# First four stages of part 0: gathered rows replaced by rows picked with one-hot matmuls (recommendation tower, 32 features)

## What is computed

```python
e = jnp.stack([tbl_0[ids[:, 0]], ..., tbl_31[ids[:, 31]]], axis=1)      # 2048 x 32 x 64
z = concatenate([sum(e, -1), einsum('bpd,pde,bpe->bp', e[:, II], kernels, e[:, JJ])], 1)   # 32 + 496
h = concatenate([z, dense_ctx], 1)
h = relu(h @ W_top1 + b_top1)      # 544 -> 512
h = relu(h @ W_top2 + b_top2)      # 512 -> 256
y = h @ W_top3                     # 256 -> 1
```

## Time and profile before

| what | value |
|---|---|
| median of 3 runs | 814.21 us (813.42 to 814.73) |
| the profiled execution | 812.35 us |
| its span, first to last instruction | 810.5 us |
| TensorE busy (PE) | 761.7 us, 94% |
| VectorE busy (DVE) | 720.8 us, 89% |
| ScalarE busy (ACT) | 681.7 us, 84% |
| GpSimd busy (POOL) | 607.3 us, 75% |
| bytes by indirect DMA, by plain DMA | 16.81 MB, 10.63 MB |

### The profile page before, as it was taken

How to read it: one execution, slowest core, us unless ns; L and a number is a source line. 1 busy time by engine, 2 the same in 40 slices (tenths; PEclk the granted TensorE clock), 3 DMA queues, 4 the chain that set the end, 5 groups by cost and what they waited for, 6 DMA issues and landing times.

```text
span 810.5 us, 20371 instructions
## 1 busy us (share of the span) xinstructions
PE 761.7 (94%) x6000; PEld 458.4 (57%) x6000; DVE 720.8 (89%) x684; ACT 681.7 (84%) x5282; POOL 607.3 (75%) x966
## 2 busy tenths in 40 slices
PE   0378989999999999999999999999999999999998
PEld 0144435565565666666666666656565665656656
DVE  0268999998999989999999989999999999999891
ACT  1057899989979999789989899799997899798993
POOL 6775888888888888888888888888868888660000
PEclk9999999999999999999999999999999999999999
DMA  4545111111111111111111111111111111110000
GB/s 136 162 134 181 27 24 26 25 26 25 26 26 25 26 25 25 26 25 25 25 27 25 25 25 26 25 25 26 24 23 24 26 25 26 20 21 2 1 2 1
DMA packets 20014, 28.74 MB, mean 35 GB/s; under 512 B 9024, under 2 KB 9664, under 8 KB 19008
## 3 DMA queue, kind: packets, MB, share of 16 engines
q0 software_dynamic: 16384, 16.81, 10.7%
q1 hardware_dynamic: 3520, 10.63, 4.0%
HBM read 27.40 MB, written 0.01 MB: 34 GB/s over the span
## 4 chain that ended last, share of the span: by engine, by line
PE 83%; DMA 6%; POOL 6%; issue 2%; ACT 2%; DVE 1%; DVEq 0%; POOLq 0%
PE m_ps L646 25%; PE m_ps L662 25%; PE acc L676 13%; PE tr L585 8%; DMA gathered<-in_tbl,idx 6%; POOL gathered L328 6%; PE tr L566 4%; PE tr L599 3%; ACT turned_act L427 1%; PE m_ps L648 1%; PE m_ps L585 1%; PE tr L580 1%; PE m_ps L599 0%; POOL x_half L311 0%; DMA idx<-in_ids 0%
## 5 line engine op out<-in xcount | busy, mean ns | idle before, releaser
L427 ACT ACTIVATE turned_act<-turned_act 128x64 f32<-128x64 f32 x2560 | 612.1, 244 | 26.3 <-DVE turned_act L513 26.2
L328 POOL DMA_INDIRECT gathered<-in_tbl,idx x512 | 489.4, 956 | 100.2 <-issue 74.4
L427 ACT ACTIVATION_READ_ACCUMULATOR turned_act<-turned_act 128x1 f32 x2560 | 486.4, 190 | 0.0
L488 DVE TENSOR_TENSOR prod<-m_ps,x_t 128x1024 f32<-128x1024 f32 x256 | 308.1, 1217 | 11.2 <-PE m_ps L648 10.7
L646 PE MATMUL m_ps<-x_t,k_sb 64*128 64x256 f32 x1024 | 271.8, 391 | 3.9 <-DVE turned_act L513 2.1
L648 PE MATMUL m_ps<-x_t,k_sb 64*128 64x256 f32 x1024 | 272.6, 392 | 0.0
L662 PE MATMUL m_ps<-k_sb,x_t 64*128 64x512 f32 x1024 | 262.7, 608 | 4.4 <-DVE turned_act L513 3.5
L646 PEld LDWEIGHTS m_ps<-x_t,k_sb 64*128 64x128 f32 x1024 | 182.4, 188 | 107.9 <-issue 63.2
L513 DVE TENSOR_TENSOR turned_act<-m_ps,gathered 128x1024 f32<-128x1024 f32 x160 | 193.4, 1217 | 25.0 <-PE m_ps L662 12.4
L648 PEld LDWEIGHTS m_ps<-x_t,k_sb 64*128 64x128 f32 x1024 | 182.1, 188 | 0.0
L662 PEld LDWEIGHTS m_ps<-k_sb,x_t 64*128 64x128 f32 x1024 | 92.6, 187 | 67.1 <-issue 43.7
(11 more groups left out here) (36 smaller groups left out, 152.6 us busy)
## 6 DMA issues: line engine op xcount, KB each, us to landing
gathered<-in_tbl,idx POOLq DMA_INDIRECT x512, 2.5
k_sb<-in_kmat SPq DMA_DIRECT2D x7, 1024.0 KB, 4.9
w_sb<-in_w SPq DMA_DIRECT2D x1, 1280.0 KB
k_sb<-in_kmat SPq DMA_DIRECT2D x2, 256.0 KB, 3.1
k_sb<-in_kmat SPq DMA_DIRECT2D x1, 512.0 KB, 5.1
w_sb<-in_w SPq DMA_DIRECT2D x1, 512.0 KB
idx<-in_ids SPq DMA_DIRECT2D x1, 256.0 KB, 2.6
z_sb<-in_dense_t SPq DMA_DIRECT2D x8, 16.0 KB, 2.1
```

The costliest lines, as they stand in the source:

```text
L328: nc.gpsimd.indirect_dma_start(out=gathered[:, t, G % GR, f * D:(f + 1) * D], out_offset=None, in_=tables[2 * (STAGES - 1 - a) + f], in_of ...
L427: last = nc.scalar.activation(row, row, ACT.Copy, accum_out=z_turned[:, q % 2, t, 16 * c + n:16 * c + n + 1])
L488: nc.vector.tensor_tensor(prod[:, r % PR, :, :].rearrange("p u (e n) -> p u e n", e=2), m_ps[:, p % MR, :, :].rearrange("p u (e n) -> p u ...
```

## The change

The rows of stages 0 to 3 of part 0 are no longer gathered. The eight tables are loaded whole, each over 125 partitions with r = 8 or 10 rows per partition (row p x r + c lies in partition p at place c). The 256 indices of a feature are loaded to all 125 partitions (`ids_hot`). For each place c, VectorE compares the indices with p x r + c (`rows_hot`, one float per partition and place) and writes a 125x256 matrix of ones and zeros; TensorE multiplies the 125x64 piece of the table with it and accumulates over c in PSUM. The result is the stage's transposed rows, in `tr` as before: feature 0 in rows 0 to 63, feature 1 in rows 64 to 127. The matrices lie in a ring of five. VectorE makes all 70 before its first product. Tables, lists and matrices lie in parts of `x_t`, `w1_sb` and `z_sb` that are not yet used; the load of `w1_sb` waits until stage 3 is picked. The sums of the four stages' rows come from eight small matmuls with `sel` (`first_sums`), whose result ScalarE copies to `z_nat`. Gathers begin with stage 4 (k = 16); counts of semaphores are adjusted.

```diff
+HOT = 4
+HOT_P = 125
+HOT_RING = 5
+TABLES_AHEAD = 3
...
+AHEAD[0, FIRST_AHEAD[HOT + 2]].append(("s", 0, 0))
...
+SIZES = (125000, 1000, 1000, 1250, 12500, 1000, 1250, 12500, 1250, 1000, 12500, 1250, 125000, 125000, 12500, 12500,
+         1000, 12500, 1000, 1250, 1000, 12500, 12500, 1250, 1000, 1250, 1000, 1000, 1000, 1250, 1000, 1250)
+HOT_R = [[SIZES[2 * (STAGES - 1 - _a) + _f] // HOT_P for _f in range(2)] for _a in range(HOT)]
+HOT_COLUMNS = sorted({(_r, _c) for _pair in HOT_R for _r in _pair for _c in range(_r)})
...
+        K0 = HOT * GATHERS
+        hot_steps = [(a, c, f) for a in range(HOT) for c in range(max(HOT_R[a])) for f in range(2) if c < HOT_R[a][f]]
+        final = {(a, f): max(j for j, e in enumerate(hot_steps) if e[0] == a) for a in range(HOT) for f in range(2)}
+        used_by = [sum(i != final[hot_steps[i][0], 0] for i in range(j + 1)) for j in range(len(hot_steps))]
+        w1_flat = w1_sb[:].rearrange("p k n -> p (k n)")
+        x_flat = x_t[:, STAGES:XR, :].rearrange("p s n -> p (s n)")
+        def hot_table(a, f):
+            home, first = (x_flat, 0) if a < TABLES_AHEAD else (w1_flat, TABLES_AHEAD)
+            at = D * (sum(sum(HOT_R[b]) for b in range(first, a)) + (HOT_R[a][0] if f else 0))
+            return home[0:HOT_P, at:at + D * HOT_R[a][f]]
+        def hot_matrix(j):
+            at = D * sum(HOT_R[HOT - 1]) + QB * (j % HOT_RING)
+            return w1_flat[0:HOT_P, at:at + QB]
+        def hot_ids(a):
+            return z_sb[0:HOT_P, a // 2, a % 2 * 2:a % 2 * 2 + 2, :].bitcast(i32)
...
-                pool.wait_ge(gather_landed[k % IN_FLIGHT], (k // IN_FLIGHT + 1) * 16)
+                pool.wait_ge(gather_landed[k % IN_FLIGHT], ((k - K0) // IN_FLIGHT + 1) * 16)
...
-            for k in range(NQ * STAGES * GATHERS):
+            for k in range(K0, NQ * STAGES * GATHERS):
...
-                if k >= IN_FLIGHT:
+                if k >= K0 + IN_FLIGHT:
...
-                if n == 0 and G >= GR:
+                if n == 0 and G >= GR + HOT:
...
             sp.dma_start(idx[:], ids).then_inc(idx_loaded, 16)
+            sp.dma_start(rows_sb[:], rows_hot).then_inc(rows_loaded, 16)
+            def load_tables(a):
+                sp.dma_start(hot_ids(a), ids_hot[a:a + 1, :].rearrange("o (f n) -> o f n", f=2).partition_broadcast(HOT_P)).then_inc(ids_hot_loaded[a], 16)
+                for f in range(2):
+                    sp.dma_start(hot_table(a, f), tables[2 * (STAGES - 1 - a) + f].rearrange("(p r) d -> p (r d)", p=HOT_P)).then_inc(tables_loaded[a], 16)
+            load_tables(0)
+            load_tables(1)
             sp.dma_start(b1_sb[:], b1).then_inc(small_loaded, 16)
             sp.dma_start(b2_sb[:], b2).then_inc(small_loaded, 16)
             sp.dma_start(w3_sb[:], w3).then_inc(small_loaded, 16)
             at = 0
             for n, size in enumerate(K_LOADS):
+                if n == 1:
+                    load_tables(2)
+                    load_tables(3)
                 if n > 2:
                     sp.wait_ge(tr_kept, 3 * (n - 2) // 2)
                 sp.dma_start(k_sb[:, at:at + size, :], kmat[:, at * P:(at + size) * P].rearrange("p (d n) -> p d n", n=P)).then_inc(k_loaded[n], 16)
                 at += size
+            sp.wait_ge(tr_filled, place("x", 0, HOT - 1))
             sp.dma_start(w1_sb[:], w1.rearrange("(k p) n -> p k n", p=P)).then_inc(weights_loaded, 16)
             sp.dma_start(w2_sb[:], w2.rearrange("(k p) n -> p k n", p=P)).then_inc(weights_loaded, 16)
...
+            def keep_first_sums():
+                act.wait_ge(tr_filled, place("s", 0, 0))
+                nc.scalar.activation(z_nat[:, 0, :, 0:2 * HOT], tr[:, 0, 0:TILES * 2 * HOT].rearrange("p (t n) -> p t n", t=TILES),
+                                     ACT.Copy).then_inc(tr_kept, 1)
...
             def sum_x(q, a, n):
                 G = q * STAGES + a
+                if q == 0 and a < HOT:
+                    return
...
+            dve.wait_ge(rows_loaded, 16)
+            for j, (a, c, f) in enumerate(hot_steps):
+                if c == 0 and f == 0:
+                    dve.wait_ge(ids_hot_loaded[a], 16)
+                if j >= HOT_RING:
+                    i = j - HOT_RING
+                    if i == final[hot_steps[i][0], 0]:
+                        dve.wait_ge(tr_filled, place("x", 0, hot_steps[i][0]))
+                    else:
+                        dve.wait_ge(hot_used, used_by[i])
+                column = HOT_COLUMNS.index((HOT_R[a][f], c))
+                nc.vector.tensor_scalar(out=hot_matrix(j), in0=hot_ids(a)[:, f, :], scalar1=rows_sb[0:HOT_P, column:column + 1],
+                                        scalar2=None, op0=ALU.is_equal).then_inc(hot_ready, 1)
...
+            def pick_rows(a):
+                free_tr("x", 0, a)
+                pe.wait_ge(tables_loaded[a], 32)
+                for j, (b, c, f) in enumerate(hot_steps):
+                    if b == a:
+                        pe.wait_ge(hot_ready, j + 1)
+                        last = nc.tensor.matmul(tr[f * D:(f + 1) * D, 0, :], hot_table(a, f)[:, c * D:(c + 1) * D], hot_matrix(j),
+                                                start=(c == 0), stop=(c == HOT_R[a][f] - 1))
+                        if j == final[a, 0]:
+                            last.then_inc(tr_filled, 1)
+                        else:
+                            last.then_inc(hot_used, 1)
+            def first_sums():
+                free_tr("s", 0, 0)
+                for t in range(TILES):
+                    for a in range(HOT):
+                        at = 2 * (HOT * t + a)
+                        last = nc.tensor.matmul(tr[:, 0, at:at + 2], x_t[:, slot(0, a), t * P:(t + 1) * P], sel[:, 30:32],
+                                                start=True, stop=True)
+                last.then_inc(tr_filled, 1)
...
             def transpose(q, a):
                 G, n = q * STAGES + a, STAGES_AT_ONCE[q]
+                if q == 0 and a < HOT:
+                    pick_rows(a)
+                    return
                 if q == 0:
                     for landed in gather_landed:
-                        pe.wait_ge(landed, (G + n) * GATHERS // IN_FLIGHT * 16)
+                        pe.wait_ge(landed, ((G + n) * GATHERS - K0) // IN_FLIGHT * 16)
                 else:
...
+                if what == "s":
+                    keep_first_sums()
...
+        "ids_hot": np.ascontiguousarray(ids[0:QB, hot].T).reshape(HOT, 2 * QB),
+        "rows_hot": np.array([[p * r + c for r, c in HOT_COLUMNS] for p in range(P)], np.float32),
```

More of the change, by code:

```diff
@@ L203, with dlrm_tower @@
 VECTOR_SUMS_BEHIND = (7, 10, 11, 12, 13, 15, 17, 18, 19, 23, 24, 25, 26, 27, 28, 29, 30, 31)
-def dlrm_tower(nc, ids, tables, kmat, dense_t, w1, b1, w2, b2, w3, out):
+SIZES = (125000, 1000, 1000, 1250, 12500, 1000, 1250, 12500, 1250, 1000, 12500, 1250, 125000, 125000, 12500, 12500,
+         1000, 12500, 1000, 1250, 1000, 12500, 12500, 1250, 1000, 1250, 1000, 1000, 1000, 1250, 1000, 1250)
+HOT_R = [[SIZES[2 * (STAGES - 1 - _a) + _f] // HOT_P for _f in range(2)] for _a in range(HOT)]
+HOT_COLUMNS = sorted({(_r, _c) for _pair in HOT_R for _r in _pair for _c in range(_r)})
+def dlrm_tower(nc, ids, ids_hot, rows_hot, tables, kmat, dense_t, w1, b1, w2, b2, w3, out):
     fp32, i32 = mybir.dt.float32, mybir.dt.int32
@@ L237, in dlrm_tower @@
         y_sb = sb("y_sb", [P, YN])
+        rows_sb = sb("rows_sb", [P, len(HOT_COLUMNS)])
         idx = sb("idx", [P, NQ * STAGES * GATHERS], i32)
@@ L255, in dlrm_tower @@
         small_loaded = sem("small_loaded")
+        rows_loaded = sem("rows_loaded")
+        ids_hot_loaded = [sem(f"ids_hot_loaded{a}") for a in range(HOT)]
+        tables_loaded = [sem(f"tables_loaded{a}") for a in range(HOT)]
+        hot_ready = sem("hot_ready")
+        hot_used = sem("hot_used")
         weights_loaded = sem("weights_loaded")
@@ L401, in keep_z @@
                 nc.scalar.activation(z_sb[:, q % 2, b, :], acc[:, 0:QB], ACT.Copy).then_inc(z_kept, 1)
+            def keep_first_sums():
+                act.wait_ge(tr_filled, place("s", 0, 0))
+                nc.scalar.activation(z_nat[:, 0, :, 0:2 * HOT], tr[:, 0, 0:TILES * 2 * HOT].rearrange("p (t n) -> p t n", t=TILES),
+                                     ACT.Copy).then_inc(tr_kept, 1)
             def keep(what, q, n):
-                if what == "x":
+                if what == "s":
+                    keep_first_sums()
+                elif what == "x":
                     keep_x(q, n)
@@ L459, in sum_x @@
                 G = q * STAGES + a
+                if q == 0 and a < HOT:
+                    return
                 if q == 0:
                     for landed in gather_landed:
-                        dve.wait_ge(landed, (G + n) * GATHERS // IN_FLIGHT * 16)
+                        dve.wait_ge(landed, ((G + n) * GATHERS - K0) // IN_FLIGHT * 16)
                     nc.vector.tensor_reduce(z_nat[:, 0, :, 2 * a:2 * a + 2],
@@ L496, in turned_product @@
```

(11 more changed lines are left out.)

6 lines of the change are left out of this document (3 added, 3 removed).

## The result

| what | before | after |
|---|---|---|
| median of 22 runs each | 813.34 us (810.46 to 815.39) | 815.13 us (812.73 to 818.31) |
| the profiled execution | 812.35 us | 815.48 us |
| its span | 810.5 us | 813.7 us |
| T, start of the first turned product | 49.09 us | 55.44 us |

The ratio is 1.0027, with a 95% interval of 1.0016 to 1.0038: slower by some 2.2 us, where 2.7 us faster was forecast.

The account below looks back on a forecast made before the run. The start-up up to T was taken as the bound: tables at 33.5 us, picking to 41.0, then 8.1 us, left T at 49.1 us, unchanged; the closed gap gave -2.7 us, so 811.5 us by the median, range 801.5 to 818.5.

Parts of the forecast that it names:

- Where the end is set: Start-up: everything behind T, the first turned product's start at 49.09 us, is the same work, so the end moves with T.
- Gap behind T: VectorE's waits between 70.89 and 74.06 us, for stage 11 and then TensorE, 2.75 us in all, would go.
- Contention: Gathers up to stage 11: 10 us allowed for slowing by other loads, within 57 us where 69.7 us would do.
- Compares and matmuls: Picking stages 0 to 3: 70 steps, each a 0.32 us compare and a matmul of 0.24 or 0.47 us.
- the chain behind it: From the end of picking at 41.0 us to T: copies, transposes, sums and multiplies in TensorE's order, 8.1 us.
- rival B: TensorE stays at half speed through stage 3 and the chain to T: T 56.1 us, time 818.5 us; chance 0.15.
- Loads: Start-up lists and tables over 125 rows: five DMA engines at 24 GB/s, stage 3's tables in at 33.5 us (31 to 37.6).
- rival A: Start-up loads use all 16 engines: picking ends at 31.3 us, T 39.4 us, time 801.8 us; chance 0.17.

## Why the prediction was wrong

**Where the end is set** held: what follows T took 758.2 to 758.4 us of the span in the changed kernel and in those with held blocks, lists over 128 and all engines. T -5.8, -8.3 and -12.4 us shortened the spans by 5.8, 8.3 and 12.3 us. With three stages T -18.0 us gave only -15.0 us (13.3 by the ratios), since VectorE waits behind T again.

**Gap behind T** held: no wait for gathers. But stage 4 and later did not come 20 us sooner. The second part's first halving started at 81.29 us, where it had been 94.38 (the chain up to 90 us is gathers in flight to 64.1%, 48.9%). Contention took 7 us; the slack given for it covered that.

**Compares and matmuls** held: 0.305 us for a taken 0.32; half speed for some ten steps and 4.5 us (40.20 to 44.74 us), where 8.5 steps and 4.0 us were forecast; sums 1.95 us for 2.0; stage 3 from start to end 7.2 us for 7.5; the chain behind it 8.06 us for 8.1. The stay at half speed (rival B) did not come: the steps behind 44.74 us are 0.31 us apart again.

**Loads: the step that failed.** "Stage 3's tables are in at 33.5 us (31 to 37.6)" (3.4 + 29.9 is 33.3, a slip of no weight): it was 40.2 us, 6.7 us later, beyond the bound. Of the 6.7 us, 4.76 were the wait of stage 3. The other 1.9 would have been there with tables in time, since TensorE was busy until 35.4 us: its first pick began at 14.28 us, where tables at about 11 us had been worked out. The number of engines, five, and their rate, 24 GB/s, were right. With all engines instead (rival A, as an edit) the time was 803.82 us, for 801.8 worked out; its picking ended at 34.99 us where 31.3 was given, because the first tables came at 8.8 and not 6.6 us, and between the picks of the four stages lay 3.9 us (1.82 and 0.47 us of waits for ScalarE's copies and 1.63 us with the first even step in it), for which 0.6 us had been given; the picks themselves took 22.2 us, 1.8 less than worked out. The Trainium skill ("DMA: Bandwidth & Descriptors", section "Why a DMA increments its semaphore by 16 and not by 1") has the number of engines as the largest up to 16 that divides the slowest dimension on both sides; by it, five for 125 rows, and the packets here agree, with 30 per 0.5 us at 84 ns.

Two sentences of that step were wrong. "SP issues 13 more transfers at 0.43 us each, the last at about 8.4 us: no bound": the last ended at 24.1 us, since SP's issue itself was held while earlier loads lay on the five engines (5.95 us; 1.64 with the lists elsewhere; none with all loads on all engines). What in the queue holds it is not shown. It delays every load that stands behind in SP's order. The start was slow besides: the core moved 93 GB/s in the first 10 us, where the all-engines kernel moved 189; why the first lists and tables ran under their later rate was not tried. And the kernel blocks were taken to lie queued behind the tables; they went beside stage 3's tables, whose packets took 131 ns instead of 84, and cost some 3.5 us by the run that held them back. With those blocks held and the shorter stop of SP the last 2,560-byte packet ends at 34.05 us and stage 3 starts at 34.7 us, 1.2 us over the forecast: in this one execution the sum by bytes nearly comes out, for five engines that are left alone.

With T at 49.1 + 6.35 us the same working gives 809.65 + 6.3 = 816.0 us for the profiled execution, which took 815.48. That the changed kernel's time lay within the range is no merit of the mechanism: it lay there on the side of rival B, by another cause, late tables and not a slow TensorE.

## What to carry to other kernels

Before a load is placed, divide its rows: 125 rows went over five engines, and here a broadcast over 128 partitions instead of 125 gave 8 us back, together with tables loaded as 112 and 13 rows 10.5 us. Cost a load with few engines twice, by its bytes over those engines and by the time for which the queue that issues it is held, and look at what is issued beside it. And with a chain like this one, find the term that decides (here one landing time), and let its bounds cover what the loads before and beside it can do to it, not only the spread of its own rate.

## What the runs showed that was not expected

- An issue of SP took up to 3 us (5.95 us for two) instead of 0.43 us when earlier loads lay on five engines. The same two tables as four loads on more engines took 1.70 us.
- The stop of SP is not the same in every execution: 5.95 us in one and 4.10 us in another, with the same code up to there.
- TensorE's granted clock fell after short idle time: in the changed kernel TensorE idled from 35.4 to 40.2 us, and the granted clock is 1.00 up to 38 us, 0.50 from 39 to 44.6 us, with picks 0.43 us a step, and 1.00 from 45.1 us on.
- It also fell with hardly any idle time. With held blocks and with lists over 128, TensorE had stood idle for at most 0.6 us at a time since its last picks; right behind the eight small matmuls of the sums the granted clock is 0.50 (from 46 to 49 us and from 44 to 46 us). From the last pick to T these two took 9.5 us, where the changed kernel and the one with all loads on all engines took 8.06. In the latter the clock stayed at 1.00 through the same instructions; why is open.
- The mean granted clock tells executions of one kernel apart. The kernel before, run beside the one with three stages, took 810.7 to 812.6 us where that clock was 1.00 and 813.5 to 813.9 us where it was 0.998. Of the changed kernel's 22 executions none had 1.00.
